# Vision tower kernel: score units in another order, keys placed in two halves, and four engines' lists rearranged

## The chip, the cores and the metric

The kernel runs on one core of one Trainium2 chip. The metric is the device time in microseconds (us), taken as the median of several executions. The core has the engines TensorE (PE in the profile, its weight loads PEld), VectorE (DVE), ScalarE (ACT), GpSimd (POOL) and SyncE (SP), which here only issues DMAs. Each engine works through its own list of instructions in order and meets the others at semaphores.

## What is computed

128 images of 3 x 224 x 224 go, each for itself, through one small transformer tower. 14 x 14 patches make T = 196 tokens of D = 192 features. There are three stages: the patch embedding with two layer norms, a causal attention of 12 heads of 16 dimensions, and a routed block in which 29 of the 196 tokens go through a second attention and the others through a mixing product, followed by an MLP of width 768. Shortened:

```python
p = img2patches(x, 16, 16); h = layernorm(layernorm(p) @ W + b)
a = layernorm(h)
q, k, v = split(a @ w_attn + b_attn)          # 12 heads
scores = q @ k.T * scale + q @ rel.T * scale  # causal mask
h = h + softmax(scores) @ v @ w_proj + b_proj
n = ln(layernorm(h)); s = sigmoid(n @ Wr + br)
merged = where(lowest 29 of s, attention(n), mix(n, s))
h2 = layernorm(h) + merged
h = h + h2 + gelu(ln(h2) @ W1) @ W2
```

## The kernel before

The loop is a software pipeline over images. One pass, `step(k, m, n, l, ...)`, does the embedding and the keys and queries of image l (`head`), the causal attention of image n (`front`), the routed block of image m (`back`) and the MLP of image k (`tail`), with k, m, n, l four neighbouring images. `steps` runs three passes that fill it, a hardware loop over 124 images, and three that empty it. Every engine has its own `step`, whose calls are written out in a fixed order; the engine does them in that order.

The causal attention of one image is cut into nine score units, S0 to S8, three for each group of four heads (`s_unit`, line 88). The first half of the tokens (t = 0) sees 98 keys, so one unit holds all four heads (slots 0 to 3, 98 wide); the second half sees 196, so there is one unit for slots 0 and 1 and one for slots 2 and 3. In each unit TensorE adds a mask and two products of `qparts` with `kz` (lines 729 and 732), VectorE takes the negated maximum (`maxima`, L1226), ScalarE does the exponentials with their sums (`softmax`, L1610), VectorE inverts the sums (`inverse_sums`, L1242) and GpSimd multiplies (`normalised`, L544). TensorE then transposes the result in nine groups A0 to A5 and B0 to B2 (L767), which VectorE (A0, A2, A3, L1234) or ScalarE (the others, L1618) copies out. A `RING` of four PSUM banks carries units and groups: each waits till the one before it in its bank is used up. A4 takes the bank of B0. Then come the products with the values (`attention`, L920 and L927) and the projection (L939).

`kz` holds the keys of each slot in an otherwise zero store; it and `qparts` are filled from `kq` by ten DMAs that SyncE issues in `place_keys` (line 423) when VectorE has written `kq`'s low part (L1219). One semaphore, `kz_in`, counts the eight DMAs of the keys, another, `q_in`, the two of the queries, which are issued last. TensorE waits for both ahead of S0.

Around it lie, on TensorE: the patch matmuls (`embed`, L743), of which the second half comes in two pieces; the products fwm (`mixing_rows`) and fwv (`values2`), both on line 687; `weighted_sum` (L891), `gather`, `qsel`, `scores2`, `transposes2` (L865) and `context2` (L875) of the routed block; `square_sums` (L753), which needs the sum of the squares from GpSimd (L561 to L565); `up` (L695) and `down` (L973) of the MLP. `up(1)` writes the bank that the embedding leaves when VectorE has made `tok_y` from it, for which GpSimd makes a reciprocal root (`rstd`). On VectorE: `rank_tokens` (L1310 to L1318), `mixing_rows` (L1328), `kept_rows` (L1336), `mix` (L1342 to L1349), `q_blocks` (L1357 and L1360), the embedding's normalisation (L1263 to L1282), `context2` with the sum over the heads. On ScalarE: the copies of the values (L1599), kk, vv (L1632), the split columns nTs and z3Ts (L1572), the copy of the routed probabilities (`transposed2`, L1657) and two table loads a pass (L1588), one for Exp and one for Gelu.

## Time and profile before

| | |
|---|---|
| median of 3 runs | 4954.72 us (4946.73 to 4960.03) |
| the profiled execution | 4944.02 us |
| its span, first to last instruction | 4942.2 us |
| TensorE matmuls | 4696.2 us busy, 95% |
| weight loads | 4299.3 us, 87% |
| VectorE | 3872.3 us, 78% |
| ScalarE | 3448.9 us, 70% |
| GpSimd | 3065.9 us, 62% |
| mean granted TensorE clock | 0.989 |

The rows come from that one profiled execution. Busy time is the time in which an engine has an instruction of the program in work; matmuls are pipelined and their ends modelled, so a busy TensorE can still wait. In a timeline row the first number is the start in us from the span's start, the second how long the row's instructions took from the first's start to the last's end, then engine, source line, operation, what is written and read, the shape, and how many instructions the row holds. A bracket names idle time before it and who ended it.

### The profile page before, as it was taken

The page shows a single profiled execution, that of the slowest core. Times are in us where ns is not written, and L with a number is a line of the kernel's source. Part 1 is how long each engine was busy: PE and PEld are TensorE (multiplying, and loading weights), DVE is VectorE, ACT ScalarE, POOL GpSimd, SP SyncE. Part 2 cuts the span into 40 slices and gives each one's busy share as a digit, 9 for nine tenths or more (in the row PEclk, how much of TensorE's full clock was granted, in tenths as well). Part 3 has the DMA queues.
Part 4 walks back from the last instruction along what each step waited for, and adds up shares of the span by engine and source line. Part 5 has one row for each costly group of instructions (what it writes and reads, how often), then busy time and mean ns, then how long its engine had stood idle before and what let it go on. Part 6 is the DMA issues. An engine that isn't in the chain of part 4 may idle for free. (4 is left out here: it accounts for less than half of the span.)

```text
span 4942.2 us, 143405 instructions
## 1 busy us (share of the span) xinstructions
PE 4696.2 (95%) x44376; PEld 4299.3 (87%) x44376; DVE 3872.3 (78%) x13015; ACT 3448.9 (70%) x12030; POOL 3065.9 (62%) x4143
## 2 busy tenths in 40 slices
PE   3899999999999999999999999999999999999998
PEld 3788888888888888888888888888888888888887
DVE  3787887887888788788788878878878877887885
ACT  1667777776776777777677677777777767767775
POOL 2566666666666666666666666666666666666664
PEclk7899999999999999999999999999999999999999
DMA  5555555455555555555555555555554555555551
GB/s 70 68 68 72 69 71 72 66 74 67 69 73 67 72 70 70 72 67 73 69 67 74 67 70 72 68 72 69 71 71 66 74 67 69 72 67 72 70 70 21
DMA packets 339085, 340.16 MB, mean 69 GB/s; under 512 B 47652, under 2 KB 306033, under 8 KB 339057
## 3 DMA queue, kind: packets, MB, share of 16 engines
q1 hardware_dynamic: 332522, 337.37, 52.3%
q10 hardware_dynamic: 6535, 2.45, 0.3%
q8 instruction: 14, 0.23, 0.0%
q14 instruction: 14, 0.11, 0.0%
HBM read 204.78 MB, written 19.27 MB: 45 GB/s over the span
## 5 line engine op out<-in xcount | busy, mean ns | idle before, releaser
L1610 ACT ACTIVATE p<-banks,negmax 98x98 f32<-98x98 f32 (+1 forms) x3072 | 1139.3, 379 | 216.9 <-issue 121.8
L544 POOL TENSOR_TENSOR p<-p,rden 98x392 f32<-98x392 f32 x1152 | 980.9, 870 | 280.8 <-DVE rden L1242 280.7
L1226 DVE TENSOR_REDUCE negmax<-banks 98x2 f32<-98x392 f32 (+1 forms) x1152 | 609.6, 557 | 141.0 <-PE banks L732 122.2
L732 PE MATMUL banks<-kz,qparts 128*98 128x392 f32 x2304 | 648.9, 385 | 0.0
L1610 ACT ACTIVATION_READ_ACCUMULATOR p<-banks,negmax 98x1 f32 x3072 | 612.0, 199 | 0.0
L743 PE MATMUL banks<-tokw,x_sb 128*98 128x193 f32 x3072 | 592.4, 336 | 15.5 <-POOLq L556 14.6
L743 PEld LDWEIGHTS banks<-tokw,x_sb 128*98 128x98 f32 x3072 | 553.9, 252 | 20.3 <-issue 14.6
L767 PE MATMUL banks<-ident,p 98*98 98x98 f32 x4608 | 530.4, 252 | 24.1 <-ACTq L1614 4.1
L695 PE MATMUL banks<-z3Ts,w_split 128*128 128x196 f32 x3840 | 508.4, 279 | 33.7 <-ACT gT L1685 32.3
L695 PEld LDWEIGHTS banks<-z3Ts,w_split 128*128 128x128 f32 x3840 | 468.2, 192 | 64.2 <-ACT gT L1685 58.0
L535 POOL TENSOR_TENSOR gparts<-gT,gparts 128x392 fp32r<-128x392 f32 x384 | 395.2, 1040 | 190.9 <-DVE gparts L1434 190.9
L767 PEld LDWEIGHTS banks<-ident,p 98*98 98x98 f32 x4608 | 410.2, 128 | 94.6 <-DVE pT L1234 39.7
L973 PE MATMUL banks<-w,gparts 128*98 128x192 f32 x4608 | 435.2, 253 | 0.2 <-POOL gparts L535 0.2
L973 PEld LDWEIGHTS banks<-w,gparts 128*98 128x98 f32 x4608 | 424.4, 164 | 0.3 <-POOL gparts L535 0.3
L1584 ACT CAST kq<-banks 128x588 fp32r<-128x588 f32 x128 | 83.4, 652 | 479.6 <-PE banks L715 479.6
L518 POOL TENSOR_TENSOR rstd<-ve,nhalf 98x2 f32<-98x2 f32 x512 | 355.9, 695 | 72.7
L732 PEld LDWEIGHTS banks<-kz,qparts 128*98 128x98 f32 x2304 | 321.9, 166 | 38.4
L1618 ACT COPY pT<-banks 98x392 f32<-98x392 f32 x768 | 332.0, 479 | 17.6 <-PE banks L767 5.4
L729 PE MATMUL banks<-tri,identh 98*98 98x196 bf16 (+1 forms) x1152 | 325.0, 282 | 7.0 <-DMA qparts<-kq 6.2
L1588 ACT ACT_TABLE_LOAD x252 | 323.3, 1283 | 4.5
L561 POOL TENSOR_TENSOR gstore<-gstore 128x588 f32<-128x588 f32 x128 | 155.4, 1214 | 243.2 <-ACT gstore L1595 243.2
L1675 ACT ACTIVATE f<-h,shift,rstdf 98x192 f32<-98x192 f32 x256 | 126.2, 541 | 228.4 <-DVE shift L1450 228.4
(264 smaller groups left out, 11542.3 us busy)
## 6 DMA issues: line engine op xcount, KB each, us to landing
x_sb<-in_x SPq DMA_DIRECT2D x384, 196.0 KB, 5.0
kz<-kq SPq DMA_DIRECT2D x1024, 73.5 KB, 2.6
x_sb<-in_x SPq DMA_DIRECT2D x256, 190.8 KB, 8.9
x_sb<-in_x SPq DMA_DIRECT2D x256, 185.5 KB, 11.1
qparts<-kq SPq DMA_DIRECT2D x256, 147.0 KB, 2.7
x_sb<-in_x SPq DMA_DIRECT2D x128, 189.0 KB, 7.3
out<-out_row SPq DMA_DIRECT2D x128, 147.0 KB
pT<-in_L_ffn_W ACTq DMA_DIRECT2D x1, 576.0 KB
```

Source lines behind the costliest of these rows:

```text
L518: gp.tensor_tensor(r, ve, nhalf[:], ALU.pow).then_inc(sem[name], 1)
L535: gp.tensor_tensor(gparts[:, 1, at], gT[:, j % 2], gparts[:, 0, at].bitcast(F32), ALU.subtract).then_inc(sem["gparts_sb"], 1)
L544: gp.tensor_tensor(heads, heads, rden[:, g, t, s0:s0 + sn].unsqueeze(2).broadcast_to([HT, sn, w]), ALU.mult).then_inc(sem["pnorm_sb"], 1)
L695: last = mm(o, w[:, wpart, lo:hi], src[:, p], start=i == 0, stop=i == len(PAIRS) - 1)
L729: mm(masked, identh[:], tri[:].unsqueeze(1).broadcast_to([HT, len(slots), HT]), start=True, stop=False, skip_group_check=True)
L732: last = mm(o, qparts[:, g, HT * t:HT * t + HT], kz[:, slots[0]:slots[-1] + 1, part, g, 0:w], start=False, stop=part == 1, skip_group_chec ...
L743: last = mm(bank[b][0:HT, t * (D + 1):(t + 1) * (D + 1)], xf[:, a:a + (HT - 1) * PS + 1:PS], tokw[:, q], start=t == 0 and q == 0, stop=q = ...
L767: last = pe.transpose(bank[b][0:HT, HT * i:HT * i + HT], src, ident[0:HT, 0:HT])
L973: last = mm(bank[7][0:HT, t * D:(t + 1) * D], gparts[:, part, f, HT * t:HT * t + HT], w2[:, wpart, f], start=f == 0 and t == 0 and i == 0, ...
L1226: ve.tensor_reduce(negmax[:, g, t, slots[0]:slots[-1] + 1], bank[RING[f"S{k}"]][0:HT, 0:w * len(slots)].rearrange("p (s w) -> p s w", w=w) ...
L1610: sc.activation((p1 if t else p0)[0:HT, 4 * g + s], bank[b][0:HT, w * i:w * i + w], ACT.Exp, bias=negmax[:, g, t, s:s + 1], accum_out=den[ ...
L1618: sc.copy(pt_dst(name[0], int(name[1:])), bank[RING[name]][0:HT, 0:4 * HT]).then_inc(sem["pT_act"], 1)
```

## The change

`s_unit` gives the units of a group in the order slots 0 and 1 of the second half, then the first half, then slots 2 and 3. `place_keys` issues the two query DMAs first, then the keys slot by slot; slots 0 and 1 count on one semaphore (`kza_in`), slots 2 and 3 on another (`kzb_in`). TensorE waits ahead of S0 for the queries and the first half of the keys, and ahead of S1 for the second half.

The lists of all four computing engines are rearranged. On TensorE S0 now stands straight behind the first patch matmuls, fwv behind S0 and fwm behind S3; attention stands ahead of attn_out, the columns of the next image and up(2). On ScalarE the values and the Exp load change places, as do the keys of the routed block with the scores' exponential, vv and the z3Ts columns come behind softmax 0, the Gelu load stands ahead of B0's copy and the gelus behind all of them. On GpSimd normalised(0) stands ahead of the sum of squares. On VectorE the ranks stand behind the maximum of S0, the mixing rows behind that of S3, and the other maxima and inversions are interleaved otherwise with the routed block. On VectorE and GpSimd the small steps at the pass's end (h2's and h3's statistics and roots) change places too. No instruction but one wait is added, and the same arithmetic is done.

```diff
--- before.py
+++ after.py
@@ -66,7 +66,7 @@
 
 SEMS = dict(
 
-    x_in=len(XROWS) * 16, out_done=16, kz_in=8 * 16, q_in=2 * 16,
+    x_in=len(XROWS) * 16, out_done=16, kza_in=4 * 16, kzb_in=4 * 16, q_in=2 * 16,
 
     tok_mm=1, sqs_mm=1, zT_mm=1, score_mm=1, mrow_mm=1, usum_mm=1, kk_mm=1, vv_mm=1, aT_mm=1, kq_mm=1, v_mm=1,
     s_mm=9, p_T=len(PT), y_mm=2, proj_mm=1,
@@ -87,7 +87,8 @@
 
 def s_unit(u):
 
-    g, part = divmod(u, 3)
+    g, j = divmod(u, 3)
+    part = (1, 0, 2)[j]
     if part:
         return g, 1, range(2 * part - 2, 2 * part), T
     return g, 0, range(4), HT
@@ -423,15 +424,15 @@
             def place_keys(n):
 
                 sp.wait_ge(sem["kqlo_sb"], after("kqlo_sb", n))
+                for part in range(2):
+                    sp.dma_start(qparts[64 * part:64 * part + 64].bitcast(F32),
+                                 kq[64:128, part].bitcast(F32)).then_inc(sem["q_in"], 16)
                 for s in range(4):
                     for r in range(2):
                         at = 64 * r + DH * s
                         sp.dma_start(kz[at:at + DH, s].bitcast(F32),
                                      kq[DH * s:DH * s + DH].bitcast(F32)).then_inc(
-                                         sem["kz_in"], 16)
-                for part in range(2):
-                    sp.dma_start(qparts[64 * part:64 * part + 64].bitcast(F32),
-                                 kq[64:128, part].bitcast(F32)).then_inc(sem["q_in"], 16)
+                                         sem["kza_in" if s < 2 else "kzb_in"], 16)
 
             prefetch(0, 1)
             sp.wait_ge(one["stores_zeroed"], 1)
@@ -556,6 +557,8 @@
                     gp.drain().then_inc(sem["xlast_sb"], 1)
                 if front:
                     h1_with_bias()
+                if front:
+                    normalised(0)
                 if head:
                     gp.wait_ge(sem["sq_sb"], after("sq_sb", l))
                     gp.tensor_tensor(x_sq[:, :, 0:3], x_sq[:, :, 0:3], x_sq[:, :, 3:6], ALU.add)
@@ -568,34 +571,32 @@
                     gp.drain()
                     gp.tensor_tensor(h2b[:], h2[:], both(bf2), ALU.add).then_inc(sem["h2b_sb"], 1)
                 if front:
-                    normalised(0)
-                if front:
                     normalised(1)
                 if front:
                     normalised(2)
                 if front:
                     normalised(3)
+                if front:
+                    normalised(4)
+                if front:
+                    normalised(5)
                 if head:
                     gp.wait_ge(sem["tok_var"], after("tok_var", l))
                     rstd(var1[:], ve1[:], rstd1[:], "tok_rstd")
-                if front:
-                    normalised(4)
-                if front:
-                    normalised(5)
                 if back:
                     gp.wait_ge(sem["rden2_sb"], after("rden2_sb", m))
                     gp.tensor_tensor(probs2[:], probs2[:],
                                      rden2[:].unsqueeze(2).broadcast_to([128, NG, T]),
                                      ALU.mult).then_inc(sem["pn2_sb"], 1)
+                if front:
+                    normalised(6)
+                if front:
+                    normalised(7)
+                if front:
+                    normalised(8)
                 if head:
                     gp.wait_ge(sem["y_stat"], after("y_stat", l))
                     rstd(mv_y[:, :, 1], ve2[:], rstd2[:], "y_rstd")
-                if front:
-                    normalised(6)
-                if front:
-                    normalised(7)
-                if front:
-                    normalised(8)
                 if head:
                     gp.wait_ge(sem["h1_stat"], after("h1_stat", l))
                     rstd(mv_a[:, :, 1], ve3[:], rstd3[:], "h1_rstd")
...
@@ -790,7 +791,9 @@
                             if back:
                                 pe.wait_ge(sem["h2_sb"], all_before("h2_sb", n))
                             pe.wait_ge(sem["q_in"], after("q_in", n))
-                            pe.wait_ge(sem["kz_in"], after("kz_in", n))
+                            pe.wait_ge(sem["kza_in"], after("kza_in", n))
+                        if k == 1:
+                            pe.wait_ge(sem["kzb_in"], after("kzb_in", n))
                         scores(k, RING[name])
                     else:
 
@@ -994,71 +997,71 @@
                     score()
                 if head:
                     embed(0,0,QX)
-                if back:
-                    mixing_rows()
+                if front:
+                    causal("S0")
+                if back:
                     values2()
                 if front:
-                    causal("S0")
                     causal("S1")
                     causal("S2")
-                if back:
+                    causal("S3")
+                if back:
+                    mixing_rows()
+                if front:
+                    causal("S4")
+                if back:
+                    gather()
                     weighted_sum()
-                if front:
-                    causal("S3")
-                if back:
-                    gather()
                 if head:
                     square_sums()
-                if front:
-                    causal("S4")
+                if back:
+                    qsel()
+                if front:
                     causal("S5")
                 if head:
                     embed(1,0,3)
-                if back:
-                    qsel()
                 if front:
                     causal("S6")
+                if back:
+                    scores2()
+                if front:
+                    causal("S7")
                 if head:
                     embed(1,3,QX)
                 if front:
-                    causal("S7")
-                if back:
-                    scores2()
-                if front:
                     causal("S8")
+                    causal("A0")
                 if tail:
                     up(0)
                 if front:
-                    causal("A0")
+                    causal("A1")
                 if tail:
                     up(1)
                 if front:
-                    causal("A1")
                     causal("B0")
-                if back:
-                    transposes2()
-                if front:
                     causal("A2")
                     causal("A3")
-                if back:
-                    context2()
-                if front:
                     causal("B1")
+                if back:
+                    transposes2()
+                if front:
                     causal("A4")
                     causal("A5")
                     causal("B2")
+                if back:
+                    context2()
+                if front:
+                    attention()
+                if back:
+                    attn_out()
+                if head:
+                    attention_cols()
                 if tail:
                     up(2)
-                if back:
-                    attn_out()
-                if head:
-                    attention_cols()
-                if front:
-                    attention()
+                if front:
+                    projection()
                 if back:
                     scatter()
-                if front:
-                    projection()
                 if head:
                     keys()
                 if tail:
@@ -1460,11 +1463,13 @@
                 if back:
                     routed_cols_lo()
                     routing_scores()
+                    sigmoid()
+                if front:
+                    maxima(0)
+                if back:
                     rank_tokens()
-                    sigmoid()
-                    mixing_rows()
-                if front:
-                    maxima(0)
+                if front:
+                    inverse_sums(0)
                     maxima(1)
                     maxima(2)
                 if tail:
@@ -1472,48 +1477,48 @@
                 if front:
                     maxima(3)
                 if back:
+                    mixing_rows()
+                if front:
+                    maxima(4)
+                if back:
                     kept_rows()
                 if front:
-                    inverse_sums(0)
                     inverse_sums(1)
                 if back:
                     mix()
+                    q_blocks()
                 if front:
                     inverse_sums(2)
-                    maxima(4)
+                    inverse_sums(3)
                     maxima(5)
-                    inverse_sums(3)
                     maxima(6)
-                if back:
-                    q_blocks()
+                    inverse_sums(4)
+                    inverse_sums(5)
+                if back:
+                    max2()
+                if front:
+                    maxima(7)
+                    inverse_sums(6)
                 if head:
                     patch_variance()
                 if front:
-                    inverse_sums(4)
-                    maxima(7)
-                if back:
-                    max2()
-                if front:
-                    inverse_sums(5)
+                    maxima(8)
+                if back:
+                    inverse2()
+                if front:
+                    transposed("A0")
                 if head:
                     embedding()
-                if back:
-                    inverse2()
-                if front:
-                    maxima(8)
-                    inverse_sums(6)
-                    transposed("A0")
-                if head:
-                    embedding_scaled()
                 if front:
                     inverse_sums(7)
                     inverse_sums(8)
                     transposed("A2")
                 if head:
+                    embedding_scaled()
+                if front:
+                    transposed("A3")
+                if head:
                     embedding_normalised()
-                if front:
-                    transposed("A3")
-                if head:
                     h1_stats()
                 if back:
                     context2()
@@ -1522,6 +1527,8 @@
                 if tail:
                     gelu_parts(0)
                     gelu_parts(1)
+                if front:
+                    attention()
                 if back:
                     attn_out()
                 if head:
@@ -1529,17 +1536,15 @@
                 if tail:
                     gelu_parts(2)
                 if front:
-                    attention()
+                    residual()
                 if back:
                     merge()
-                if front:
-                    residual()
+                if head:
+                    keys()
+                if front:
+                    routed_input()
                 if back:
                     mlp_input()
-                if head:
-                    keys()
-                if front:
-                    routed_input()
                 if tail:
                     output()
             step(-3, -2, -1, 0, True, False, False, False, False)
@@ -1689,24 +1694,25 @@
                 if back:
                     routed_cols_hi()
                 if front:
+                    load_table(ACT.Exp)
                     values()
-                    load_table(ACT.Exp)
-                if back:
+                if head:
+                    squares()
+                if back:
+                    exp_scores()
                     keys2()
-                    exp_scores()
-                if head:
-                    squares()
+                if front:
+                    softmax(0)
+                if back:
+                    values2()
                 if tail:
                     mlp_cols_hi()
-                if back:
-                    values2()
-                if front:
-                    softmax(0)
+                if front:
                     softmax(1)
+                    softmax(2)
                 if back:
                     gathered()
                 if front:
-                    softmax(2)
                     softmax(3)
                 if back:
                     queries2()
@@ -1720,25 +1726,26 @@
                     softmax(7)
                     softmax(8)
                     transposed("A1")
-                if back:
-                    transposed2()
-                if front:
-                    transposed("B0")
                 if tail:
                     load_table(ACT.Gelu)
-                    gelu(0)
-                    gelu(1)
+                if front:
+                    transposed("B0")
+                if back:
+                    transposed2()
                 if front:
                     transposed("B1")
                     transposed("A4")
                     transposed("A5")
                     transposed("B2")
+                if tail:
+                    gelu(0)
+                    gelu(1)
+                if front:
+                    attention()
                 if head:
                     attention_cols_hi()
                 if tail:
                     gelu(2)
-                if front:
-                    attention()
                 if head:
                     keys()
                 if front:
```

## Rows read from the trace of the kernel before

**Rows 1.** Windows: us, busy (and count) by engine, clock, DMA share, GB/s; two passes
```profile
2500.00:2537.40 37.40, 36.31 (x348) 33.28 (x348) 29.99 (x102) 26.95 (x94) 23.85 (x33) 1.00 0.55 70
2537.40:2574.80 37.40, 36.30 (x348) 33.28 (x348) 29.99 (x102) 26.96 (x94) 23.86 (x33) 1.00 0.56 70
```

**Rows 2.** Waits of TensorE's weight loads: total us, times, longest us
```profile
PEld banks L875 <- ACT scratch L1657: 65.5, 128, 1.2
PEld banks L695 <- ACT gT L1685: 58.0, 128, 1.9
```

**Rows 3.** Timeline of TensorE in one pass: start us, us, line, tiles, count, idle before
```profile
2541.00 0.50 PE L679 MATMUL banks<-ident,z 98*128 98x98 f32 x4
...
2546.41 1.19 PE L687 MATMUL banks<-fwm_split,nTs 128*98 128x192 f32 x10
...
2548.33 0.33 PE L729 MATMUL banks<-tri,identh 98*98 98x392 bf16 x1
...
2564.12 1.09 PE L875 MATMUL banks<-scratch,vv 98*64 98x128 f32 x12 [0.31 <-ACT scratch L1657]
2565.14 1.87 PE L767 MATMUL banks<-ident,p 98*98 98x98 f32 x16
...
2567.25 1.36 PE L695 MATMUL banks<-z3Ts,w_split 128*128 128x196 f32 x10 [0.24 <-ACT gT L1685]
...
2572.00 1.31 PE L939 MATMUL banks<-wps,yparts 128*98 128x192 f32 x12 [0.23 <-DVE yparts L1417]
...
2578.40 0.50 PE L679 MATMUL banks<-ident,z 98*128 98x98 f32 x4
```

**Rows 4.** SyncE's DMA issues ahead of the same pass, and their landing (us)
```profile
2539.45 4.99 SPq L429 DMA_DIRECT2D kz<-kq  x8
2544.48 1.23 SPq L433 DMA_DIRECT2D qparts<-kq  x2
...
DMA to landing us min/median/max: 2.4/2.6/2.7
```

**Rows 5.** Timeline of VectorE in the same pass
```profile
2545.78 0.42 DVE L1310 SCALAR_TENSOR_TENSOR scratch<-zclip,zi,tie 98x196 f32<-98x196 f32 x1
...
2547.63 0.56 DVE L1328 TENSOR_TENSOR mrow<-banks,b1m 98x384 f32<-98x384 f32 x1 [0.23 <-PE banks L687]
...
2549.06 1.51 DVE L1226 TENSOR_REDUCE negmax<-banks 98x4 f32<-98x392 f32 x3 [0.87 <-PE banks L732]
...
2554.48 1.02 DVE L1226 TENSOR_REDUCE negmax<-banks 98x2 f32<-98x392 f32 x2
...
2556.18 0.60 DVE L1357 TENSOR_TENSOR qb<-qs,slot_of 128x256 f32<-128x256 f32 x1
```

**Rows 6.** Timeline of ScalarE in the same pass
```profile
2549.66 0.34 ACT L1610 ACTIVATE p<-banks,negmax 98x98 f32<-98x98 f32 x1 [0.65 <-DVE negmax L1226]
...
2556.62 0.42 ACT L1610 ACTIVATE p<-banks,negmax 98x196 f32<-98x196 f32 x1 [0.16 <-issue]
...
2563.20 0.86 ACT L1657 COPY scratch<-banks 98x384 f32<-98x384 f32 x2
2563.95 0.51 ACT L1618 COPY pT<-banks 98x392 f32<-98x392 f32 x1
2564.47 1.28 ACT L1588 ACT_TABLE_LOAD   x1
```

**Rows 7.** Timeline of GpSimd in the same pass: first and last of the squares' sums
```profile
2547.18 1.22 POOL L561 TENSOR_TENSOR gstore<-gstore 128x588 f32<-128x588 f32 x1 [1.83 <-ACT gstore L1595]
...
2549.24 0.72 POOL L565 TENSOR_TENSOR sqsum<-gstore 128x196 f32<-128x196 f32 x1
```

**Rows 8.** Two VectorE lines over the execution: ns min/median/max, first and last start
```profile
L1346 DVE SCALAR_TENSOR_TENSOR wkeep<-sig,rss,keep x128: 221/516/521, 158.4 to 4907.9; 98x2 f32<-98x2 f32 x128
...
L1282 DVE SCALAR_TENSOR_TENSOR h<-y_row,rstd,ln2b x256: 407/556/998, 92.4 to 4845.6; 98x192 f32<-98x192 f32 x128
```

More of the change, by code:

```diff
@@ L577, in step @@
                     normalised(3)
-                if head:
-                    gp.wait_ge(sem["tok_var"], after("tok_var", l))
-                    rstd(var1[:], ve1[:], rstd1[:], "tok_rstd")
                 if front:
@@ L584, in step @@
                     normalised(5)
+                if head:
+                    gp.wait_ge(sem["tok_var"], after("tok_var", l))
+                    rstd(var1[:], ve1[:], rstd1[:], "tok_rstd")
                 if back:
@@ L589, in step @@
                                      ALU.mult).then_inc(sem["pn2_sb"], 1)
-                if head:
-                    gp.wait_ge(sem["y_stat"], after("y_stat", l))
-                    rstd(mv_y[:, :, 1], ve2[:], rstd2[:], "y_rstd")
                 if front:
@@ L598, in step @@
                     normalised(8)
+                if head:
+                    gp.wait_ge(sem["y_stat"], after("y_stat", l))
+                    rstd(mv_y[:, :, 1], ve2[:], rstd2[:], "y_rstd")
                 if head:
@@ L607, in step @@
                     gelu_low(2)
-                if back:
-                    gp.wait_ge(sem["h3_stat"], after("h3_stat", m))
-                    rstd(mv_3[:, :, 1], ve5[:], rstd5[:], "h3_rstd")
                 if front:
@@ L619, in step @@
                         sem["f_rstd"], 1)
+                if back:
+                    gp.wait_ge(sem["h3_stat"], after("h3_stat", m))
+                    rstd(mv_3[:, :, 1], ve5[:], rstd5[:], "h3_rstd")
                 if back:
@@ L1035, in step @@
                 if front:
-                    causal("A1")
                     causal("B0")
+                    causal("A2")
+                    causal("A3")
+                    causal("B1")
                 if back:
@@ L1502, in step @@
                 if front:
-                    maxima(8)
-                    inverse_sums(6)
                     transposed("A0")
                 if head:
-                    embedding_scaled()
+                    embedding()
                 if front:
@@ L1516, in step @@
                 if head:
+                    embedding_normalised()
                     h1_stats()
```

33 lines of the change are left out of this document (14 added, 19 removed).

## Prediction

> **What bounds the kernel now.** I read the windows view first, for the period. Two neighbouring stretches of 37.40 us, one pass of the loop each, look the same: TensorE busy 36.3 us, VectorE 30.0, ScalarE 27.0, GpSimd 23.9, the clock at its full level [rows 1]. So the time is about 127 passes of 37.40 us (4750 us) and some 190 us of filling and emptying, and what counts is what a pass becomes. TensorE is the fullest engine but not gapless. The table of waits gives its weight loads two long ones: 65.5 us over 128 passes for ScalarE's copy of the routed probabilities, 58.0 us for a gelu [rows 2]. That is 0.5 us a pass each.
>
> Then I laid the four engines' timelines of one pass side by side. All times t below are us after 2541.00, where TensorE starts a pass; it starts the next at 37.40 [rows 3]. The chain that I take to carry the pass runs through the attention of one image: its nine score units, the maximum of each on VectorE, its softmax on ScalarE, the division on GpSimd, the transposes, the context. Score unit 0 starts at t 7.33; its softmax starts at 2549.66, and from there ScalarE works nearly without a gap for 14.8 us until it has copied the transposes B0 out (2563.95 + 0.51) [rows 3, 6]. The last transposes wait for such copies.
>
> **Part 1, unit 0 earlier.** Two blocks of ten matmuls, fwm and fwv, fill t 5.41 to 7.33 [rows 3]. Now unit 0 stands ahead of both. Of the 1.92 us I put 0.13 down to the join behind the patch matmuls, an estimate, and 0.9 to each block; the join stays, so unit 0 starts at t 5.54. Its maximum began 0.73 after its start [rows 3, 5]; a unit of two slots streams its first matmul over half as many columns, so I take 0.65, t 6.2. That is 1.9 us earlier than before.
>
> **Part 2, the placement.** SP starts placing at t -1.55 (2539.45, the copy before the pass) and issues 8 DMAs in 4.99 us, 0.62 each; the landing takes 2.4 to 2.7 us [rows 4]. With the two query DMAs and slots 0 and 1 first, unit 0 needs the sixth: issued at t 1.57, landed by 4.3, hidden by 1.2 us. Unit 1 needs the tenth: issued at 4.07, landed at 6.7 to 6.8. Unit 1 comes behind unit 0 (0.44) and fwv (0.9), at t 6.88. It is hidden by 0.1 us only; if it isn't, unit 1 is late, but VectorE, busy with the ranks, takes unit 1 only at 8.1, so up to 0.5 us more costs nothing. Without the split, unit 0 would wait for 6.8. Behind the added wait on TensorE stand units 1 to 3. The ten DMAs are the same, and what follows them on SP (the store, later the prefetch) moves by nothing.
>
> **Part 3, VectorE behind unit 0.** Before, the six maxima of units 0 to 5 with what lay between them (z3T's low part, kept rows, mix) took 2549.06 to 2555.50, 6.44 us [rows 5]. The same six now have more between them: the ranks (2545.78 to the end of their two last small operations, 1.3 us), the mixing rows (0.5 of 0.56 us), the q blocks (0.7 of the 0.60 us operation and its smaller partner) and one reciprocal [rows 5]. So the sixth maximum, unit 5's, ends at 6.2 + 6.44 + 1.3 + 0.5 + 0.7 + 0.2 = t 15.35. Before, unit 5's softmax began at 2556.62, t 15.62 [rows 6]; now it can at 15.4. Of the 1.9 us won at unit 0, 0.2 are left here. On the way two waits fall on TensorE: weighted_sum for the mixing rows (0.2 us), and square_sums. For the latter GpSimd's normalised(0), 0.84 us, now stands ahead of the sum of squares; that takes 2547.18 to 2549.96, 2.8 us [rows 7], so it can't end before t 8.2 (unit 0's sums inverted behind the ranks: 6.2 + 0.55 + 1.3 + 0.15) + 0.85 + 2.8 = 11.9, and TensorE is there at 11.6: 0.3 us, which makes qsel and so queries2 on ScalarE late by the same. ScalarE's slack takes it up, since softmax 5 waits for 15.35 anyway.
>
> **Part 4, ScalarE.** From the softmax of unit 5 (2556.62 is its first ACTIVATE) to the end of B0's copy (2563.95 + 0.51) ran 7.84 us, with the copy of the routed probabilities inside (0.74 of 0.86 us) [rows 6]. The list keeps these items, moves that copy behind B0's and the gelu table load ahead of it: 1.28 us and a dummy activation, 1.41 us from 2564.47 [rows 6]. 7.84 - 0.74 + 1.41 + 0.15 for one more wait = 8.65 us. B0 is out at t 15.4 + 8.65 = 24.05, against 23.46 before. A4 needs B0's bank. TensorE itself would be at A4 at about 23.6, even after 0.5 us for the embedding that it awaits ahead of up(1), because the patches' second half and hence tok_y are 2 us later; so B0 decides.
>
> **Part 5, TensorE to the end of the pass.** From A4 on: three groups of transposes (16 took 1.87 us with a wait inside; 0.35 a group), context2 (2564.12 to 2565.14, 1.02), and then the same work that ran from 2567.25 to 2578.40, 11.15 us, in another order [rows 3]. In that stretch projection had waited 0.3 us for yparts and the head-wise products 0.1 [rows 3]; attention now stands far ahead of projection, with attn_out, the columns and up(2) between, so both go: 10.75. The gelu and the routed copy are done before they are asked for, which removes the two long waits of [rows 2]. attn_out now waits for VectorE's head sums, 0 to 0.3 us (0.2). Sum: 24.05 + 1.05 + 1.02 + 10.75 + 0.2 = 37.07; I add 0.1 for small joins. **37.15 us a pass, 0.25 less.** Times 127 that is 32 us; filling and emptying have the same work, cost at nothing with 5 us either way. The profiled execution took 4944.0 us (its span 4942.2), so 4912; the median of the three runs shown, 4954.7, is 10.7 above it, so **4923 us**.
>
> So an earlier start of 1.9 us and some 1.3 us of removed waits are swapped for a fuller VectorE and a table load on the chain. No operation is new; what the trace of before can't show is which VectorE and GpSimd operations will now lie side by side. Its price is bounded by nothing below (mix is stretched already) and 0.6 us above (rival a); I take nothing, since one such meeting goes for each new one as far as I can see.
>
> **A rule that speaks against it.** A VectorE operation on 98x2 elements, of mix, took 516 ns in the median and 221 at least; one of 98x192 took 407 to 998 ns [rows 8]. The longest ones lie beside GpSimd tensor_tensor operations. The Trainium skill (GPSIMD Engine Reference, Key points) says that GpSimd shares its SBUF interfaces with VectorE and contends with VectorE instructions that have two SBUF inputs. By that rule kept rows, which ran while GpSimd was idle, would be stretched now that sums of squares and h2b run beside them, and the time would be that of the first rival; the trace agrees with the rule as far as rows 8 go.
>
> **Rivals.** (a) *VectorE is held by GpSimd.* Kept rows (two operations with two SBUF inputs) and mix lie at t 11.4 to 13.9; GpSimd then runs the sum of squares, h2b and normalised(1), where it had stood idle beside kept rows. One stretched operation costs 0.3 (516 - 221) to 0.6 us (998 - 407) [rows 8], and it lies on the chain of part 3. At +0.25 the gain is gone; at +0.6 a pass is 37.75: 4955 + 0.35 x 127 = **4999**, at +0.45 **4980**. For: the chain there has no slack. Against: mix already pays once. 0.22. (b) *The same time*: gain and new waits cancel within 0.12 us a pass, **4955**. 0.20. (c) *ScalarE runs through.* If VectorE keeps ahead, ScalarE starts 1.9 us earlier than at 2549.66, does the 14.8 us to B0's end, plus 1.41 - 0.74 and two more copies that came before unit 0 (0.9, estimated from the routed copy's 0.86): B0 out at t 8.66 - 1.9 + 14.8 + 1.6 = 23.15, a pass 36.25, 1.15 less: **4809**. For: VectorE's gaps are short. Against: part 3 finds three waits. 0.13. (d) *The split does not do what it says*: unit 1 waits for slots 2 and 3 past t 7.4, each 0.1 us later costing up to 0.1: needs landings of 3.3 us against 2.7. 0.02, near **4960**.
>
> **How the numbers follow.** The forecast (a pass 0.12 to 0.7 us shorter, 4865 to 4940) has 0.43. About 0.3%, 15 us, is what a measurement of this kernel can tell from no change. Faster: 0.43 + 0.13 + 0.01 = 0.57; same 0.20; slower 0.23. The range takes the forecast, (b) and most of (a), and cuts (c) in its lower half: 4845 to 4990.
>
> **What would show it.** Unit 0 about 1.9 us earlier in the pass and no wait on kz or qparts: part 2. Unit 5's maximum ending near t 15.4, with VectorE without idle time from 6.2 on: part 3. TensorE waiting at A4 for ScalarE's B0, near 0.5 us, at square_sums 0.3 and at up(1) 0.5: parts 3 and 4. No wait left for the routed copy, the gelu or yparts: part 5. Wrong would be: kept rows or mix longer than in [rows 8] (rival a); ScalarE gapless from t 6.8 to 23 (rival c); a new wait that I haven't listed in the second half, where h1's normalisation, GpSimd's roots and the head sums follow each other closely.

## The result, and the profile after

The changed kernel takes 4961.6 us (median of 20 runs), the kernel before 4953.6 us (20 runs): a ratio of 1.0015, 95% interval 1.0008 to 1.0022. I had forecast 4923 us, 0.6% less. The time is the same by the bound of 0.3%, and a little longer within it.

In two passes of the changed kernel, by the windows view (us, busy time and count of TensorE, its weight loads, VectorE, ScalarE, GpSimd, then the clock), the answer to [rows 1]:

```profile
2511.59:2549.10 37.51, 36.06 (x348) 33.10 (x347) 30.41 (x101) 26.99 (x95) 23.06 (x32) 1.00 0.55 70
2549.10:2586.61 37.51, 36.06 (x348) 33.09 (x347) 30.39 (x101) 27.00 (x95) 23.07 (x32) 1.00 0.55 70
```

A pass is 37.51 us, 0.11 more than before, not 0.25 less. VectorE is busy 0.4 us longer for the same 102 or so instructions, which is the first hint. (The clock column is the granted TensorE clock: 1.00 is 2.4 GHz, 0.50 is 1.2 GHz.) I number times t again from the pass's start, here 2549.10. TensorE's timeline, which answers [rows 3]:

```profile
2554.68 0.25 PE L730 MATMUL banks<-tri,identh 98*98 98x196 bf16 x1
...
2564.78 0.60 PE L859 MATMUL banks<-kk,qb 128*128 128x196 f32 x2 [0.39 <-DVE qb L1363]
...
2570.42 1.33 PE L696 MATMUL banks<-z3Ts,w_split 128*128 128x196 f32 x10 [0.58 <-DVE y_row L1266]
...
2573.99 1.22 PE L768 MATMUL banks<-ident,p 98*98 98x98 f32 x12 [0.23 <-ACT pT L1623]
```

Score unit 0 starts at t 5.58, where I had put 5.54. The waits at the routed copy, the gelu and yparts are gone. In their place TensorE waits for `tok_y` ahead of up(1), for the q blocks, for B0's copy ahead of A4 and for the sum of squares ahead of square_sums, in this order in the table of its weight loads' waits (total us, times, longest):

```profile
PEld banks L696 <- issue: 94.1, 125, 0.8
PEld banks L859 <- DVE qb L1363: 88.1, 121, 1.3
PEld banks L768 <- ACT pT L1623: 57.8, 120, 0.8
PEld banks L754 <- POOL sqsum L568: 55.2, 128, 1.7
```

Now VectorE and GpSimd around kept rows (L1339), to be read beside [rows 5, 7]:

```profile
2559.91 0.56 DVE L1229 TENSOR_REDUCE negmax<-banks 98x4 f32<-98x392 f32 x1
2560.56 1.80 DVE L1339 SCALAR_TENSOR_TENSOR f<-mrow,keep,f 98x192 f32<-98x192 f32 x2
...
2564.79 1.01 DVE L1229 TENSOR_REDUCE negmax<-banks 98x2 f32<-98x392 f32 x2
```

```profile
2560.28 0.71 POOL L568 TENSOR_TENSOR sqsum<-gstore 128x196 f32<-128x196 f32 x1
2561.15 1.00 POOL L572 TENSOR_TENSOR h2b<-h,bf 98x384 f32<-98x384 f32 x1 [0.16 <-issue]
```

Kept rows start at t 11.46, where rival (a) of the prediction has them (11.4), but take 1.80 us instead of 0.75. The first of the two operations takes 0.65 us and ends 0.2 us after the sum of squares, the second takes 1.23 us and ends at 2562.36, 0.2 us after GpSimd's h2b (2562.15). What hangs on them is late by 0.9 us, the softmax of unit 5 and B0's copy:

```profile
2563.95 0.21 ACT L1615 ACTIVATION_READ_ACCUMULATOR p<-banks,negmax 98x1 f32 x1
2565.36 0.43 ACT L1615 ACTIVATE p<-banks,negmax 98x196 f32<-98x196 f32 x1 [1.21 <-DVE negmax L1229]
...
2572.07 1.28 ACT L1593 ACT_TABLE_LOAD   x1
2573.37 0.20 ACT L1593 ACTIVATE table_out<-ones 1x1 f32<-1x1 f32 x1
2573.48 0.46 ACT L1623 COPY pT<-banks 98x392 f32<-98x392 f32 x1
```

The softmax starts at t 16.26 (forecast 15.4), B0 is out at 24.84 (24.05). ScalarE stood idle for 1.21 us ahead of unit 5, waiting for VectorE.

### The profile page after: what moved, and what is told of

The parts are those of the page before. It is cut to its first block and busy times, and to the rows that moved or that the text cites. A ratio compares the mean times of both kernels' runs of the same rounds, so it can differ in the third digit from the quotient of the medians.

```text
span 4960.1 us, 143405 instructions
## 1 busy us (share of the span) xinstructions
PE 4680.2 (94%) x44376; PEld 4291.8 (87%) x44376; DVE 3922.5 (79%) x13015; ACT 3455.0 (70%) x12030; POOL 2967.1 (60%) x4143
## 5 line engine op out<-in xcount | busy, mean ns | idle before, releaser
L545 POOL TENSOR_TENSOR p<-p,rden 98x392 f32<-98x392 f32 x1152 | 947.2, 840 | 779.8 <-DVE rden L1245 777.1
L1229 DVE TENSOR_REDUCE negmax<-banks 98x2 f32<-98x392 f32 (+1 forms) x1152 | 621.0, 557 | 115.8 <-PE banks L733 111.8
L733 PE MATMUL banks<-kz,qparts 128*98 128x392 f32 x2304 | 669.5, 387 | 0.0
L744 PE MATMUL banks<-tokw,x_sb 128*98 128x193 f32 x3072 | 602.7, 340 | 15.5 <-POOLq L557 14.6
L768 PE MATMUL banks<-ident,p 98*98 98x98 f32 x4608 | 482.3, 250 | 32.8 <-ACT pT L1623 27.8
L768 PEld LDWEIGHTS banks<-ident,p 98*98 98x98 f32 x4608 | 409.8, 128 | 75.1 <-ACT pT L1623 57.8
L1690 ACT ACTIVATE gT<-banks,bf 128x196 f32<-128x196 f32 x768 | 273.0, 438 | 83.7 <-PE banks L696 83.7
L1237 DVE COPY pT<-banks 98x392 f32<-98x392 f32 x384 | 213.7, 557 | 108.5 <-PE banks L768 99.1
```

Of the source, the lines that this page charges most:

```text
L545: gp.tensor_tensor(heads, heads, rden[:, g, t, s0:s0 + sn].unsqueeze(2).broadcast_to([HT, sn, w]), ALU.mult).then_inc(sem["pnorm_sb"], 1)
L733: last = mm(o, qparts[:, g, HT * t:HT * t + HT], kz[:, slots[0]:slots[-1] + 1, part, g, 0:w], start=False, stop=part == 1, skip_group_chec ...
L744: last = mm(bank[b][0:HT, t * (D + 1):(t + 1) * (D + 1)], xf[:, a:a + (HT - 1) * PS + 1:PS], tokw[:, q], start=t == 0 and q == 0, stop=q = ...
L768: last = pe.transpose(bank[b][0:HT, HT * i:HT * i + HT], src, ident[0:HT, 0:HT])
L1229: ve.tensor_reduce(negmax[:, g, t, slots[0]:slots[-1] + 1], bank[RING[f"S{k}"]][0:HT, 0:w * len(slots)].rearrange("p (s w) -> p s w", w=w) ...
```

## Experiments

The theory, H: a VectorE operation that reads two SBUF tensors isn't finished while a GpSimd tensor_tensor runs beside it; h2b thereby costs the chain 1 us. The rival, R: kept rows are slow for what they read. A second pair came up on the way: C, that a row of thin matmuls lets the TensorE clock fall, against G, that other gaps or the pass's length do it. Each ratio is to the kernel before on the same chip. "A pass" is the median distance between two starts of the z0 transposes.

### Moving h2b

`e1_h2b_first`, on the changed kernel:

```diff
                 if front:
                     h1_with_bias()
+                if back:
+                    gp.drain()
+                    gp.tensor_tensor(h2b[:], h2[:], both(bf2), ALU.add).then_inc(sem["h2b_sb"], 1)
                 if front:
                     normalised(0)
...
-                if back:
-                    gp.drain()
-                    gp.tensor_tensor(h2b[:], h2[:], both(bf2), ALU.add).then_inc(sem["h2b_sb"], 1)
```

> The changed kernel with GpSimd's h2b (98x384, 1.0 us) taken from behind the sum of squares to ahead of normalised(0), where GpSimd stood idle for 4 us. Theory H (a VectorE operation with two SBUF inputs is not finished while a GpSimd tensor_tensor runs): the two operations of kept rows take 0.75 to 1.0 us together instead of 1.80; unit 5's maximum ends 0.8 us earlier in the pass; the pass is 36.8 to 36.9 us instead of 37.5, since the embedding's tok_y comes next; 4880 us, ratio to the kernel before 0.985. Theory R (kept rows are slow for what they read, the mixing rows just written or f0): kept rows still take 1.8 us and the time stays at 4960, ratio 1.001.

4936.6 us, ratio 0.9981 (0.9969 to 0.9994). Kept rows fell to 0.98 us together: with h2b away the second operation takes 0.41 us, while the first, still beside the sum of squares, takes 0.65. 74 passes took 36.7 us. That is H, to 0.1 us. But 49 passes took 38.2 to 38.3, which neither theory had: in each the granted clock fell to 1.2 GHz for a stretch, and the time is 1% above the 4880 us that H gave. In the loop of the kernel before it fell in none, in the changed kernel in 5 passes.

`e2_pool_as_before` has the sum of squares, h2b and normalised(0) in this order, as in the kernel before:

> The changed kernel with GpSimd's order of the kernel before at one place: sum of squares, h2b, then normalised(0). Theory H: kept rows are free (0.75 us) and square_sums no longer waits, but h2b now runs at t 7.3 to 8.3 beside the second operation of the ranks, which has two SBUF inputs too and stands on the same chain: that one takes 1.2 us instead of 0.42. The gain is passed back: a pass of 37.2 to 37.5 us, 4920 to 4960. Theory R: the ranks keep 0.42 each, kept rows stay at 1.8, only the 0.4 us of square_sums may go: 4910 to 4960 with kept rows long.

5119.4 us, ratio 1.0364 (1.033 to 1.0399). Kept rows were free (416 ns), and now the ranks were held, as expected. VectorE and GpSimd in one pass:

```profile
2546.60 0.68 DVE L1313 SCALAR_TENSOR_TENSOR scratch<-zclip,zi,tie 98x196 f32<-98x196 f32 x1
...
2547.22 1.24 DVE L1313 SCALAR_TENSOR_TENSOR scratch<-zclip,zi,tie 98x196 f32<-98x196 f32 x1
```

```profile
2546.35 0.72 POOL L566 TENSOR_TENSOR sqsum<-gstore 128x196 f32<-128x196 f32 x1
2547.23 1.01 POOL L570 TENSOR_TENSOR h2b<-h,bf 98x384 f32<-98x384 f32 x1 [0.16 <-issue]
```

The first ends at 2547.28, 0.21 after the sum of squares, the second at 2548.46, 0.22 after h2b: the same pattern on another operation with other inputs, so R is out. A pass at full clock took 37.5 us, the upper end of what was expected; the time is 3% above the 4960 us expected at most, since 59 of 123 passes had such clock stretches and took 38.9 to 40.6 us.

`e3_squares_n0_h2b` puts the sum of squares first, then normalised(0), then h2b:

> The changed kernel with the sum of squares ahead of normalised(0), and h2b behind it, so that GpSimd is idle or nearly so beside the ranks' second operation and beside kept rows. Theory H: kept rows 0.75 us, the ranks' first operation 0.1 to 0.3 us longer, no wait at square_sums; unit 5's maximum near t 15.4 to 15.6; a pass of 36.6 to 36.8 us, 4850 to 4875 us, ratio 0.982. This is what my prediction's sum becomes when the overlap is taken away. Theory R: kept rows 1.8 us, 4920 to 4960.

4889.0 us, ratio 0.9885 (0.9868 to 0.9901), above the 4850 to 4875 us that H gave. Its VectorE in one pass (start of the pass 2435.01):

```profile
2446.69 0.75 DVE L1339 SCALAR_TENSOR_TENSOR f<-mrow,keep,f 98x192 f32<-98x192 f32 x2
...
2449.87 1.01 DVE L1229 TENSOR_REDUCE negmax<-banks 98x2 f32<-98x392 f32 x2
```

Kept rows take 0.75 us; the ranks' first operation, now beside the sum of squares, takes 0.66 us instead of 0.42, as expected; unit 5's maximum is done at t 15.4, where the prediction had it; a pass is 36.68 us. The clock stretches are there too, in 23 passes of 38.1 to 38.2 us, and they make up the difference in time.

`e7_h2b_halves` cuts the suspected cost in two, on the changed kernel:

```diff
-                    gp.tensor_tensor(h2b[:], h2[:], both(bf2), ALU.add).then_inc(sem["h2b_sb"], 1)
+                    gp.tensor_tensor(h2b[:, 0], h2[:, 0], bf2[:], ALU.add)
                 if front:
                     normalised(1)
+                if back:
+                    gp.tensor_tensor(h2b[:, 1], h2[:, 1], bf2[:], ALU.add)
+                    gp.drain().then_inc(sem["h2b_sb"], 1)
```

> The changed kernel with h2b on GpSimd cut into two operations of 98x192 (0.5 us each), the second one behind normalised(1). Theory H (the second operation of kept rows ends about 0.2 us after GpSimd's operation beside it does): the two operations of kept rows take 1.3 us together instead of 1.8, unit 5's maximum is 0.3 to 0.5 us earlier, 4900 to 4930 us if the clock holds as in the changed kernel. Theory R (they are slow for another reason): 1.8 us as before, 4960.

```profile
2486.39 1.40 DVE L1342 SCALAR_TENSOR_TENSOR f<-mrow,keep,f 98x192 f32<-98x192 f32 x2
```

```profile
2486.98 0.59 POOL L572 TENSOR_TENSOR h2b<-h,bf 98x192 f32<-98x192 f32 x1 [0.16 <-issue]
```

GpSimd's operation is 0.41 us shorter, kept rows 0.40, and a pass at full clock 0.41: 37.11. So kept rows take 1.80, 1.40 and 0.98 us for h2b at 1.00 us, at 0.59 us and away (e1), and the pass follows one to one: 37.52, 37.11 and 36.70 us. (In e3 kept rows shed another 0.23 us, but the ranks took it on, and the pass stayed at 36.7.) The time, 4961.8 us (ratio 1.0027, 1.0017 to 1.0037), isn't what I expected (4900 to 4930): 49 passes with a clock stretch took the 52 us back.

### The clock

Windows of e7: a pass without and one with the stretch, then two windows of 4 us inside the second (the last three columns: clock, DMA share, GB/s):

```profile
2474.93:2512.03 37.10, 36.05 (x349) 33.12 (x348) 29.97 (x101) 26.97 (x95) 23.24 (x33) 1.00 0.56 71
2512.03:2550.23 38.20, 37.35 (x348) 34.40 (x347) 29.90 (x101) 26.98 (x95) 23.25 (x33) 0.96 0.51 69
2522.00:2526.00 4.00, 3.90 (x30) 3.22 (x29) 3.69 (x10) 2.94 (x16) 3.18 (x6) 0.88 0.00 0
2526.00:2530.00 4.00, 4.00 (x19) 3.62 (x18) 2.64 (x11) 2.60 (x15) 2.43 (x4) 0.70 0.00 0
```

And what TensorE did ahead of it:

```profile
2521.91 0.88 PE L843 MATMUL banks<-sel,z 98*128 98x32 f32 x8
2522.72 0.34 PE L846 MATMUL banks<-ident,sel 98*32 98x98 f32 x2
2522.97 0.90 PE L897 MATMUL banks<-mrow,sig 98*98 98x193 f32 x4
2523.96 0.51 PE L757 MATMUL banks<-ones,sqsum 128*98 128x1 f32 x4
2524.33 1.08 PE L854 MATMUL banks<-nsel,fwq 128*128 128x32 f32 x8
...
2526.18 2.13 PE L747 MATMUL banks<-tokw,x_sb 128*98 128x193 f32 x6
...
2530.23 1.17 PE L747 MATMUL banks<-tokw,x_sb 128*98 128x193 f32 x6
```

Six patch matmuls take 2.13 us at 2526.18 and 1.17 us at 2530.23, where the clock is back. Ahead of the fall stand gather, weighted_sum, square_sums and qsel, mostly of 1 and 32 columns. The change brought them together: before, units 3, 4 and 5 and six patch matmuls stood among them. In all six kernels with such stretches, every fall in the loop begins in or just behind this row: 12.2 to 13.7 us into the pass, and 14.2 to 14.8 us in `e4_no_split` below, whose row comes 1.5 us later. Then `e5_s5_between` takes e3 and puts one score unit back among them:

```diff
                 if back:
                     gather()
+                if front:
+                    causal("S5")
+                if back:
                     weighted_sum()
                 if head:
                     square_sums()
                 if back:
                     qsel()
-                if front:
-                    causal("S5")
```

> The kernel of e3_squares_n0_h2b with score unit 5 (two matmuls of 392 columns) moved on TensorE from behind qsel to between gather and weighted_sum. In e3 most passes took 36.7 us, but 23 of 127 took 38.1 to 38.2, and in each of those the granted clock was at 1.2 GHz for a stretch that begins some 13 us into the pass, where gather, weighted_sum, square_sums and qsel (32, 193, 1 and 32 columns) stand in a row behind a wait. Theory C (these thin matmuls in a row let the clock fall): with unit 5 among them few or no passes are long, nearly all take 36.6 to 36.7 us, 4845 to 4865 us, ratio 0.981. Theory G (the clock falls for the waits in the second half, at up(1) and A4, which stay): as many long passes as in e3, 4885 us.

4854.3 us, ratio 0.9813 (0.9796 to 0.9829): 124 passes of 36.6 to 36.7 us and no stretch at 1.2 GHz in the loop. The waits at up(1) and A4 stayed (94.5 and 57.8 us in all, 84.8 and 47.5 in e3), so G is out for them. `e10_halves_s5` does the same to e7:

> The kernel of e7_h2b_halves with score unit 5 between gather and weighted_sum on TensorE, as in e5. In e7 a pass at the full clock took 37.1 us, but 48 passes had a stretch at 1.2 GHz near 13 us into the pass and took 38.2 to 38.3. Theory C (the thin matmuls in a row let the clock fall): no such stretch in the loop, every pass at 37.1 us, 4905 to 4915 us, ratio 0.992 against e7's 1.003. If the fall hangs on the pass's length rather than on that row of matmuls: as many as in e7, 4960 us.

4908.2 us, ratio 0.9917 (0.99 to 0.9934); 124 passes of 37.1 us, none with a stretch. The pass is as long as e7's full-clock pass, so it isn't the length. C holds in both pairs. But the block put among them also took most of their waits away: 49.1 us in all at weighted_sum in e3 became 1.0 in e5, and 55.2 us at square_sums in e7 became 12.0 in e10. So whether the few columns or these waits count more is open. The number of stretches doesn't follow the length of the pass: at 37.5 us there were 5 (changed kernel) and 59 (e2), at 36.7 us 23 (e3) and 49 (e1). e2, with the most, also waits longest in the row, 150.5 us in all at weighted_sum.

### The other terms

`e4_no_split` waits for both halves of the keys ahead of unit 0:

```diff
                             pe.wait_ge(sem["kza_in"], after("kza_in", n))
-                        if k == 1:
                             pe.wait_ge(sem["kzb_in"], after("kzb_in", n))
```

> The changed kernel with TensorE waiting for both halves of the keys ahead of unit 0 (the split's purpose undone, all else kept). If unit 0's time carries the pass, unit 0 starts at t 6.8 instead of 5.6 and the pass grows by about as much, 38.4 to 38.7 us: 5075 to 5110 us, ratio 1.027. If something else carries it (the patches' second half and tok_y, on TensorE alone), the time stays within 0.5% of 4960.

5177.2 us, ratio 1.0464 (1.0447 to 1.0482), above the 5075 to 5110 us expected. TensorE in one pass that starts at 2503.35:

```profile
2506.80 2.29 PE L744 MATMUL banks<-tokw,x_sb 128*98 128x193 f32 x12
2510.42 0.26 PE L730 MATMUL banks<-tri,identh 98*98 98x196 bf16 x1 [1.33 <-DMA kz<-kq]
```

The median pass is 39.05 us, 1.5 longer, and unit 0 starts at t 7.10 in the median, 1.5 later: one to one. The prediction's landing of the tenth DMA, t 6.7 to 6.8, was 0.1 to 0.2 too early (6.93 in this pass), and unit 0 starts 0.1 to 0.2 behind it. A third of the passes took 39.6 to 39.9 with a clock stretch. So unit 0's start does carry the pass, and the split is worth 1.5 us a pass.

`e8_start_alone` gives the kernel before only the units' order, the placement, the two semaphores and

```diff
+                if front:
+                    causal("S0")
                 if back:
                     mixing_rows()
                     values2()
                 if front:
-                    causal("S0")
                     causal("S1")
```

> The kernel before with the named part of the change alone: the units' new order, queries placed first, the two semaphores, and unit 0 ahead of fwm and fwv on TensorE; the lists of the other engines as before. If unit 0's start carries the pass alone, it is 1.0 us or more shorter, 4820. I expect little of it: VectorE takes unit 0's maximum only behind the mixing rows (fwm, done near t 7.0), ScalarE its softmax only behind vv, so the softmax starts at t 8.3 to 8.4 instead of 8.66: a pass of 37.1 to 37.4 us, 4910 to 4950, ratio 0.993 to 1.000.

5037.4 us, ratio 1.0179 (1.0162 to 1.0196): slower, where I had expected a small gain. Unit 0's softmax began at t 8.35, as expected, 0.3 earlier than before. But unit 3 now has two slots, ScalarE is through it sooner, and waits for qsel (ScalarE's timeline, pass from 2511.27):

```profile
2525.31 0.45 ACT L1565 ACTIVATE qs<-banks,fbqs 128x32 f32<-128x32 f32 x2 [0.64 <-PE banks L851]
```

Behind that the longer unit 7 comes late, and both operations of h's normalisation are now held by GpSimd (0.84 and 0.99 us, before 0.41 and 1.00). The named part of the change is a loss of 1.8% without the rest of the lists. That these two make up the whole 0.7 us a pass (38.10 against 37.40) is read from one timeline, not tried.

`e6_b0_first` takes e5 and copies B0 ahead of the gelu load:

```diff
-                if tail:
-                    load_table(ACT.Gelu)
                 if front:
                     transposed("B0")
+                if tail:
+                    load_table(ACT.Gelu)
```

> The kernel of e5_s5_between with ScalarE's copy of B0 moved ahead of the gelu table load (part 4 of the change undone in part). If the load ahead of B0 carries the pass, the wait of A4's weight loads for ScalarE (0.4 us in e3) goes and the pass is 0.3 to 0.4 us shorter than in e5. If ScalarE's whole list carries it, up to B2's copy, TensorE waits at attention instead: the pass is within 0.1 us of that of e5, and the time within 0.3% of it. I expect the second.

4842.9 us, ratio 0.9787 (0.9771 to 0.9804), 0.24% below e5; a pass takes 36.62 us. B0 was out 1.3 us earlier (t 22.7 against 24.0), yet the pass is only 0.03 shorter. The wait of A4 for ScalarE (57.8 us in e5) went, and one of 41.9 us for VectorE's copy took its place. The wait at attention for ScalarE's last copy stayed as it was (21.3 us; 22.0 in e5), and so did the one at up(1) (95.0 us). By the table of waits (TensorE's weight loads):

```profile
PEld banks L768 <- DVE pT L1238: 41.9, 126, 0.3
...
PEld banks L923 <- ACT pT L1624: 21.3, 124, 0.2
```

So B0's copy alone does not carry the pass here, as expected; but the wait at attention, which I had expected to take its place, did not grow. What carries the pass now no run shows.

This is the fastest version: 2.1% below the kernel before, 2.3% below the changed one.

`e9_one_input` asks whether an operation with one SBUF tensor is held too, on e6:

```diff
                     ve.wait_ge(sem["f0_sb"], after("f0_sb", m))
+                    ve.tensor_tensor(sigkeep[:], sig[:], keep[:], ALU.mult)
...
-                    ve.scalar_tensor_tensor(wkeep[:], sig[:], rss[:], keep[:], ALU.mult, ALU.mult)
+                    ve.tensor_scalar(wkeep[:], sigkeep[:], rss[:], None, ALU.mult)
```

> The kernel of e6_b0_first with mix's 98x2 operation, sig x rss x keep (two SBUF tensors and a scalar, 0.58 us beside normalised(1) on GpSimd, 0.22 at least), made into two: sig x keep ahead of kept rows, where GpSimd is idle, and a tensor_scalar with one SBUF tensor in mix. Theory H, in the form that one-input operations are not held: the one in mix takes 0.15 to 0.2 us, unit 5's maximum is 0.2 to 0.3 us earlier (the added operation costs 0.1 to 0.15), the pass 36.3 to 36.5 us instead of 36.6, 4810 to 4840 us. If one-input operations are held too: 0.5 us for it, the pass 0.1 us longer than in e6, 4855 us.

4855.5 us, ratio 0.9809 (0.9793 to 0.9826), a pass of 36.66 us. VectorE and GpSimd:

```profile
2432.49 0.58 DVE L1352 TENSOR_SCALAR wkeep<-sigkeep,rss 98x2 f32<-98x2 f32 x1
```

```profile
2432.21 0.84 POOL L546 TENSOR_TENSOR p<-p,rden 98x392 f32<-98x392 f32 x1 [2.11 <-DVE rden L1247]
```

The one-tensor operation takes 0.58 us too (0.23 at least, in the passes that fill the pipeline) and ends at 2433.07, as GpSimd's does (2433.05). My form of H, that two inputs are needed, falls. The Trainium skill (GPSIMD Engine Reference, Key points) names both: VectorE instructions with two SBUF inputs or in a two-port performance mode. The trace agrees for this float32 tensor_scalar from SBUF to SBUF; which mode it ran in no row here shows.

Not every meeting costs something. In the changed kernel VectorE's reciprocals from SBUF to SBUF took 0.15 to 0.17 us beside GpSimd's normalised, as they did alone. And two operations with two SBUF tensors each, in h's normalisation, kept 0.42 us beside GpSimd's reciprocal root on 98x2 elements:

```profile
2573.13 0.75 DVE L1276 SCALAR_TENSOR_TENSOR y_row<-y_row,mv_y,ln2g 98x192 f32<-98x192 f32 x2
```

```profile
2573.38 0.71 POOL L519 TENSOR_TENSOR rstd<-ve,nhalf 98x2 f32<-98x2 f32 x1
```

They end at 2573.88, 0.2 us ahead of GpSimd's. Every stretched operation above met a GpSimd operation of 192 to 392 elements a partition; no run varies this size alone.

## Why the prediction was wrong

**Part 1 and part 2 held.** Unit 0 starts at t 5.58 (5.54), and there is no steady wait for `kz` or `qparts` (7.9 us in all, in 22 waits); e4 shows the price of the opposite. The waits foreseen at square_sums, A4 and up(1) came, with 0.43, 0.48 and 0.75 us each time by the table of waits, against 0.3, 0.5 and 0.5; the one for the q blocks was not on the list.

**Part 3 failed in one term.** Up to kept rows VectorE's chain ran to 0.1 us as summed. The unseen overlap, for which I took nothing on the ground that such meetings would come and go, cost 1.05 us (1.80 against 0.75). It had been laid open as rival (a), at the right place and by the right mechanism, but priced at 0.3 to 0.6 us and with a chance of 0.22. The price was taken from the stretch of one operation; kept rows are two behind each other: the first was held 0.2 us by the sum of squares, the second 0.8 us by h2b, over its whole length. The pattern that would have given it stands in the trace of the kernel before (VectorE, then GpSimd):

```profile
2563.99 1.32 DVE L1282 SCALAR_TENSOR_TENSOR h<-y_row,rstd,ln2b 98x192 f32<-98x192 f32 x2
```

```profile
2563.32 2.69 POOL L544 TENSOR_TENSOR p<-p,rden 98x392 f32<-98x392 f32 x3
```

The second h operation takes 1.00 us and ends at 2565.31, 0.2 us after the second of GpSimd's three (2565.10). So the price is what is left of GpSimd's operation, up to its 1.0 us, not a difference of VectorE's own durations. That meeting did go in the changed kernel (h takes 0.74 us there), as the prediction hoped, but it had cost VectorE 0.6 us outside the chain of part 3, and the new one cost 1.05 us on it.

**Part 4 held as a duration.** From unit 5's softmax (t 16.26) to B0's end (24.84) 8.58 us, against 8.65.

**Part 5 was too long by 0.45.** From B0's end (t 24.84) to the end of the pass it took 12.67 us; I had 1.05 + 1.02 + 10.75 + 0.2 + 0.1 = 13.1. No wait for the head sums came. The work that had run in the 11.15 us of [rows 3] takes 10.46 us, 0.3 less than my 10.75; by the windows view TensorE was busy for 10.92 us of it before and for 10.46 now, and what made the busy part shorter I haven't found. So the two errors, +0.8 at B0 and -0.45 behind it, leave 37.15 + 0.36 = 37.51.

**The sum was right but for that term and the tail**: with all but 0.2 us of the overlap away, B0 is out at t 24.0 and a pass is 36.7 (e1, e3). Times 127 that is some 89 us below the kernel before, of which the clock let e3 keep 57 and e5, after its repair, 92.

**What no part had** is the clock. It is a small thing in the changed kernel (5 passes, some 4 us) but weighs heavily in e1, e2, e3 and e7. I read the clock as 1.00 in [rows 1] and never asked what the new order of TensorE would do to it.

**The rivals.** (b), the same time, at 0.20, is what came, by way of (a): the gain and one new wait happened to cancel. Had part 5 taken the time that I gave it, a pass would have been 37.96 us, 0.56 longer than before. And the measured time lies in the stated range only because that took in (b) and most of (a). (c) stayed out of reach: even e6 stands at 36.6, not at 36.25. (d) was no issue.

## What to carry to other kernels

A list moved on one engine changes which operations of VectorE and GpSimd lie side by side. When VectorE carries the chain, lay GpSimd's long operations beside VectorE's reads of PSUM or its idle time, and price each new meeting of SBUF operands at what is left of GpSimd's operation. Look also at which matmuls a new order puts in a row: here four thin blocks in a row came with the falls of the clock, and with one score unit among them there were none. And when an order has been worked out, take it as a whole or not at all: its headline move alone was 1.8% slower.

## What the runs showed of the hardware

- VectorE's scalar_tensor_tensor and one tensor_scalar on SBUF tensors ended 0.0 to 0.2 us after a large GpSimd tensor_tensor beside them: 0.41 became 1.23 (kept rows), 0.42 became 1.24 (ranks), 0.22 became 0.58 (98x2, with one tensor or two). Maxima, which read PSUM, kept their 0.55 us in all of them; reciprocals of SBUF operands kept 0.15 to 0.17 us, and two-tensor operations beside GpSimd's 98x2 root kept 0.42 us.
- With gather, weighted_sum, square_sums and qsel in a row the granted clock fell to 1.2 GHz in 5 (the changed kernel), 23 (e3), 41 (e4), 49 (e1, e7) and 59 (e2) of some 123 passes; a pass with it is 0.7 us (changed kernel, e4) to 1.6 us (e1) longer, in e2 up to 3.1. With a score unit of 392-column matmuls among them it never did in the loop (e5, e10).
